# One direction per head group instead of two: regrouping the graph-attention heads of a fused fp32 kernel

## The chip, the core and the metric

The kernel runs on one core of a Trainium2 chip. The metric is device time in microseconds (us) of one launch. The engines are TensorE (PE, matrix products, with its weight loads listed apart as PEld), VectorE (DVE), ScalarE (ACT), GpSimd (POOL) and SyncE (SP), which here issues transfers.

## What is computed

Two layers are applied in a row to x of 2 x 2048 x 512 fp32. The first is a transformer block (adaptive layer norm, 16-head attention over 2048 rows, a feed-forward part). The second is a graph attention, and it is the one that the change touches. For each of two directions d, every row attends to the first 20 rows of its batch, with 16 heads of 32 features:

```python
kv = self_feat[:, :ng]                                   # ng = 20
qh = (self_feat @ Wq.T + bq).reshape(B, N, H, dh)
kh = (kv @ Wk.T + bk).reshape(B, ng, H, dh)
aff = jnp.einsum('bnhd,bmhd->bnhm', qh, kh) * (1.0 / np.sqrt(dh))
aff = jnp.where(mask, aff, NEG) + label_bias[:, :, None, :]
w = jax.nn.softmax(aff, axis=-1)
out_t = jnp.einsum('bnhm,bmf->bnhf', w, kv)
out = jnp.einsum('bnhf,hgf->bnhg', out_t, Wout) + bout.reshape(H, F // H)
...
for d in range(2):
    output = output + _gat_attention(...)                # W, mask and bias of direction d
return exp_v + jax.nn.relu(output)
```

## The kernel before

The program is one long list of instructions for each engine, written out by hand; semaphores order the engines against each other. Its stages are the projections, the attention, the output projection, the feed-forward part, a lead-in of the graph attention (`*_graph_shared`) and then the graph attention itself (`*_graph`) in 32 tiles of 128 rows. The first stages take the time up to about 2915 us and are the same in both kernels, apart from a few small POOL instructions behind the last of them.

The lead-in folds the weights. `out_t` is linear in kv, so for each head the 20 rows of kv times that head's block of Wout can be made once: a matrix `vw` of (head, direction, node) rows by 32 columns per head. A tile then needs only softmax weights times `vw`. Several heads are done in one matmul: `vw` is block-diagonal over the heads of a group, its off-diagonal part cleared by a mask `bm`. A group of `HG` before is 3 or 2 heads with both directions, 40 rows per head (120 or 80 rows, 96 or 64 columns); six groups make 16 heads.

To build `vw` (`VW` loop of `pe_graph_shared`, L1468), kv is laid out in `kvr` with zeros for the other direction, and each group is eight matmuls: four for the weights of direction 0 (`woT`) and four for those of direction 1 (`wcT`). Twelve groups (two batches of six) are made, three after each of the four blocks of `pe_gg`, which make the folded scores (L1427, L1436, L1439). DVE masks each group from a PSUM bank into `vw` (L1510); two banks take turns.

In a tile t the PE does, in this order: scores of tile t+1 (`pe_score`, L1598 and L1602), the transposes of tile t's softmax weights (`pe_turn_w`, L1623), the transposes of x of tile t+2 (L1581), the linear part of tile t+1 (`pe_self`, L1611 and L1613), a small transpose (L1588) and the heads of tile t (`pe_heads`, L1632): weights transposed in `wT` as the stationary operand, `vw` as the moving one. Between scores and transposes lies the softmax: DVE adds the edge term and takes the maximum (L1747, L1753), POOL subtracts (L1798), ACT takes exp (L1700), DVE sums and inverts (L1758, L1762), POOL scales (L1801). ACT copies the transposed weights to `wT` (`act_turn_w`, L1680), and DVE adds the tile's result to x (L1768).

The score tile is laid out as (head, direction, node) before. Scores and the linear part are in fp32r, a single pass; the heads, `vw` and the folding are in fp32. The trace records each fp32 matmul as two matmuls with a weight load each, so the six heads matmuls of a tile stand there as x12, and eight of a `VW` group as 16.

Of the kernel before, what the change touches and what calls it, by code (L numbers as in the profile page):

```python
# [17 lines left out]
NK = D // 128  # L18
# [13 lines left out]
TRI = ((0, 0), (0, 1), (1, 0))  # L32
HG = ((0, 3), (3, 3), (6, 3), (9, 3), (12, 2), (14, 2))
EARLY = 84
# [113 lines left out]
def program(nc, a):  # L148
# [16 lines left out]
    with ExitStack() as ctx:  # L165
# [865 lines left out]
        rows = early("rows", 4, B, D + 640, dt=F32R)  # L1031
        brow, bm = early("brow", 3, D), early("bm", 120, 96)
        wbB, m4, sel, onb = early("wbB", 128, 12), early("m4", 128, 4), early("sel", 4, 2), early("onb", 3, 4)
# [4 lines left out]
        khT = early("khT", 128, 2, NK, NB)  # L1038
        kvr = early("kvr", 128, 2, B, NK, 3, 2, NG)
        khb = early("khb", 128, 2, B, NK, 4 * NG)  # L1040
# [55 lines left out]
        def pe_graph_start(f):  # L1096
# [27 lines left out]
            elif f in (7, 8):  # L1124
                b = f - 7
                if b == 0:
                    pe.wait_ge(s_prep, 5)
                    pe.wait_ge(s_qtc, 1)
                else:
                    pe.wait_ge(s_kv, 3)  # L1130
                for k in range(NK):
                    pe.matmul(ps[0:4, 7 - b, :], lc[:, b, k, :], wcT[:, k, :], start=(k == 0), stop=False)
                pe.matmul(ps[0:4, 7 - b, :], onb, brow, start=False, stop=True).then_inc(s_rowm, 1)
            elif f == 9:
                pe.wait_ge(s_rlo, 1)
                pe_kh(0, 7)
            elif f in (10, 11):
                for kin in (2 * f - 20, 2 * f - 19):
                    if kin == 0:
                        pe.wait_ge(s_rlo, 4)  # L1140
                    elif kin == 1:
                        pe.wait_ge(s_kh, 2)
                    elif kin == 2:
                        pe.wait_ge(s_gmd, 1)
                    else:
                        pe.wait_ge(s_gma, 1)
                    pe_gm(0, 0, kin, 6 + kin % 2)
# [148 lines left out]
        def pool_graph_start(f):  # L1296

            if f == 1:
                pool.memset(lc[:, :, :, 2:4], 0.0).then_inc(s_prep, 1)
                pool.memset(lq, 0.0).then_inc(s_prep, 1)  # L1300
                pool.memset(lb[:, :, :, 0:2], 0.0).then_inc(s_prep, 1)
                pool.memset(kvr.rearrange("p d b k h e n -> p (d b k h e n)"), 0.0).then_inc(s_prep, 1)
            elif f == 2:
                pool.wait_ge(s_small, 16 * NSMALL)
                pool.tensor_copy(lc[:, :, :, 0:2], condT2.rearrange("p k b -> p b k").unsqueeze(3)
                                 .to_broadcast([128, B, NK, 2])).then_inc(s_prep, 1)
                pool.tensor_copy(lb[:, :, :, 2:4], colb[:, 1:3, :].unsqueeze(3)
                                 .to_broadcast([128, 2, NK, 2])).then_inc(s_prep, 1)
            elif f == 6:
                kvT4 = kvT.rearrange("p k (b n) -> p k b n", b=B)  # L1310
                pool.wait_ge(s_kv, 3)
                pool.wait_ge(s_prep, 4)
                for b in range(B):
                    for d in range(2):
                        pool.tensor_copy(kvr[:, d, b, :, :, d, :], kvT4[:, :, b, :].unsqueeze(2)
                                         .to_broadcast([128, NK, 3, NG])).then_inc(s_prep, 1)
                pool.tensor_copy(lq[:, :, :, 0:2], qtT.rearrange("p k b -> p b k").unsqueeze(3)
                                 .to_broadcast([128, B, NK, 2])).then_inc(s_prep, 1)
                pool.wait_ge(s_prep, 11)
                for b in range(B):  # L1320
                    pool.tensor_copy(lq[:, b, :, 2:4], colb[:, 0, :].unsqueeze(2)
                                     .to_broadcast([128, NK, 2])).then_inc(s_prep, 1)
# [83 lines left out]
        wvp = place("wvp", [128, 2, NK, D], held, F32R)  # L1406
        vw = place("vw", [120, B, 6, 96], held + 16384)
        after_vw = held + 16384 + 4 * B * 6 * 96
        gg = [place(f"gg{b}", [128, 2, NK, 640], at2 + 24576 + 20480 * b, F32R)[:, :, :, :] for b in range(B)]
        GM = [(0, 1, k, (5, 6, 7, 5)[k]) for k in range(NK)] + [(1, n // 4, n % 4, 4 + n % 3) for n in range(8)]  # L1410
        VW = [(b, q) for b in range(B) for q in range(6)]

        def pe_gg(d, b):
            n = 2 * d + b
            if n == 0:
                pe.wait_ge(s_gma, 2)
                pe.wait_ge(s_gmd, 2)
                pe.wait_ge(s_cw_nat, n_cw)
                pe.wait_ge(s_prep, 13)
            else:  # L1420
# [22 lines left out]
        def pe_graph_shared():  # L1443
            ff_over(pe)
            pe_kh(1, 4)
            for n, (d, b, kin, bank) in enumerate(GM):
# [4 lines left out]
                pe_gm(d, b, kin, bank)  # L1451
            for nv, (b, q) in enumerate(VW):
                if nv % 3 == 0:
                    pe_gg(nv // 6, nv // 3 % 2)
                h0, nh = HG[q]
                rr, cc, i = 40 * nh, 32 * nh, 4 + nv % 2
                if nv == 0:
                    pe.wait_ge(s_gmd, 8)
                    pe.wait_ge(s_prep, 10)
                    pe.wait_ge(s_cw_o0, n_cw)  # L1460
                    pe.wait_ge(s_cw_o1, 16)
                if nv == 1:
                    pe.wait_ge(s_gma, 8)
                if nv >= 2:
                    pe.wait_ge(s_vw, nv - 1)
                for d in range(2):
                    for k in range(NK):
                        m = pe.matmul(ps[0:rr, i, 0:cc], kvr[:, d, b, k, 0:nh, :, :], woT[d][:, k, 32 * h0:32 * h0 + cc],  # L1468
                                      start=(d == 0 and k == 0), stop=(d == 1 and k == 3))
                m.then_inc(s_vwm, 1)  # L1470
# [20 lines left out]
        def dve_graph_shared():  # L1491
# [6 lines left out]
            dve.tensor_tensor(wvp[:, 1, :, :], wvT, wvp[:, 0, :, :].bitcast(F32), ALU.subtract).then_inc(s_wvl, 1)  # L1498
            for nv, (of, q) in enumerate(VW):
                n = nv // 3  # L1500
                d, b = divmod(n, 2)
                if nv % 3 == 0:
                    for kv_ in range(NK):
# [3 lines left out]
                    dve_rows(2 + n, b, 6 + b, D + 320 * d, 320)  # L1507
                rr, cc = 40 * HG[q][1], 32 * HG[q][1]
                dve.wait_ge(s_vwm, nv + 1)
                dve.tensor_tensor(vw[0:rr, of, q, 0:cc], ps[0:rr, 4 + nv % 2, 0:cc], bm[0:rr, 0:cc],  # L1510
                                  ALU.mult).then_inc(s_vw, 1)
# [104 lines left out]
        def pe_turn_w(t):  # L1616
            pe.wait_ge(s_w, t + 1)
            for i in range(2):
                if t:
                    pe.wait_ge(s_wT, 3 * (t - 1) + 2 * i + 1)  # L1620
                for q in range(3):
                    h0, nh = HG[3 * i + q]
                    m = pe.transpose(ps[0:40 * nh, 5 + i, 128 * q:128 * q + 128],  # L1623
                                     ex[:, t % 2, 40 * h0:40 * (h0 + nh)], ident[:, :])
                m.then_inc(s_tw, 1)

        def pe_heads(t):
            b, j = t // (NT // B), t % 2
            for q, (h0, nh) in enumerate(HG):
                if q % 3 == 0:  # L1630
                    pe.wait_ge(s_wT, 3 * t + 2 * (q // 3) + 1)
                m = pe.matmul(ps[:, 3 + j, 32 * h0:32 * (h0 + nh)], wT[0:40 * nh, j, q, :],  # L1632
                              vw[0:40 * nh, b, q, 0:32 * nh], start=False, stop=(q == 5), skip_group_check=True)
            m.then_inc(s_hd, 1)
# [40 lines left out]
        def act_turn_w(t):  # L1675
            for r0, q0, q1 in ((120, 0, 3), (120, 3, 4), (80, 4, 6)):
                act.wait_ge(s_tw, 2 * t + q0 // 3 + 1)
                if t >= 2:
                    act.wait_ge(s_hd, t - 1)
                act.activation(wT[0:r0, t % 2, q0:q1, :],  # L1680
                               ps[0:r0, 5 + q0 // 3, 128 * (q0 % 3):128 * (q0 % 3 + q1 - q0)].rearrange(
                                   "p (q n) -> p q n", n=128), ACT.Copy).then_inc(s_wT, 1)

# [55 lines left out]
        def dve_soft1(t):  # L1739
            j = t % 2  # L1740
            a4 = af[:, j, :].rearrange("p (h d m) -> p h d m", d=2, m=NG)
            dve.wait_ge(s_score, 2 * t + 2)
# [3 lines left out]
            for d in range(2):  # L1746
                dve.tensor_tensor(a4[:, :, d, :], ps[:, 1 + d, 0:320].rearrange("p (h m) -> p h m", m=NG),  # L1747
                                  c2[:, j, 20 * d:20 * d + 20].unsqueeze(1).to_broadcast([128, H, NG]),
# [91 lines left out]
def lay_out(i):  # L1840
    g = {k: np.asarray(v) for k, v in i.items()}
    mask = g["mask_BxSxSx11_ik0"]
    adj = np.stack([mask[:, :, :NG, :], mask[:, :NG, :, :].transpose(0, 2, 1, 3)], axis=2)
    bm = np.zeros((120, 96), np.float32)
    for h in range(3):
        bm[40 * h:40 * h + 40, 32 * h:32 * h + 32] = 1.0
    m4 = np.zeros((128, 4), np.float32)
# [38 lines left out]
```

## Time and profile before

| what | value |
|---|---|
| median of 3 runs | 3323.95 us (3314.75 to 3324.57) |
| the profiled execution's own time | 3324.57 us |
| its span | 3323.3 us |
| PE busy over the span | 3203.7 us, 96% |
| DVE, ACT, POOL busy | 62%, 42%, 44% |
| mean granted clock of the PE | 0.98 of full speed |
| lead-in of the graph attention | 2929.4 to 2993.9 us |
| 29 of its 32 tiles | 3016.88 to 3306.5 us |

Busy shares are means over stages. Whether an engine sets the time of a stage is read from the chain of work that ended last, which is followed back from the last instruction: a piece of that chain is time that nothing else hid. The granted clock is the share of full speed that the PE was given; it has two levels, 2.4 GHz (1.00) and 1.2 GHz (0.50), and a value between them is a stretch with some of both.

### The profile page before, as it was taken

How to read it: one execution, taken by the hardware profiler on the slowest of the kernel's cores; microseconds unless marked ns; L12 is line 12 of the kernel's file. 1: busy time of each engine (PE TensorE's matmuls, PEld its weight loads, DVE VectorE, ACT ScalarE, POOL GpSimd, SP SyncE). 2: the span in 40 equal slices, each digit the busy share in tenths (PEclk: the TensorE clock that was granted, in tenths of full speed). 3: DMA queues.
4: the chain of work that ended last, by engine and by line, in shares of the span. 5: the costliest groups of instructions: out<-in, count | busy, mean ns of one | idle time of the engine just before them, and what ended most of it. 6: DMA issues, size and time to landing. Idle time of an engine off the chain costs nothing.

```text
span 3323.3 us, 44389 instructions
## 1 busy us (share of the span) xinstructions
PE 3203.7 (96%) x16890; PEld 2185.3 (66%) x16890; DVE 2072.6 (62%) x3524; ACT 1394.6 (42%) x2707; POOL 1471.1 (44%) x665
## 2 busy tenths in 40 slices
PE   8799999999999999999999996899999999999999
PEld 7677655555555555555555533678888888778888
DVE  4647778778788787887878753833333333226766
ACT  2121466666666666666666663311111111112322
POOL 0200478768777777787777865400000000002222
PEclk9899999999999999999999998999999999999999
DMA  5474588888979888798797857801111111311221
GB/s 196 147 220 138 146 202 186 190 193 187 210 175 204 194 179 203 180 203 194 175 197 186 180 135 205 288 19 39 38 39 39 38 38 40 102 34 64 73 77 58
DMA packets 186171, 466.22 MB, mean 140 GB/s; under 512 B 27196, under 2 KB 69308, under 8 KB 154215
## 3 DMA queue, kind: packets, MB, share of 16 engines
q0 software_dynamic: 32256, 234.90, 31.7%
q1 hardware_dynamic: 153703, 228.49, 23.2%
q8 instruction: 133, 2.18, 0.3%
q14 instruction: 79, 0.65, 0.1%
HBM read 151.90 MB, written 75.76 MB: 69 GB/s over the span
## 4 chain that ended last, share of the span: by engine, by line
PE 84%; DMA 8%; DVE 4%; issue 1%; ACT 1%; POOL 1%; SPq 0%; DVEq 0%; POOLq 0%; ACTq 0%
PE ps L359 13%; PE ps L621 13%; PE ps L633 12%; PE ps L1075 11%; PE ps L1064 11%; DMA accd<-pt 5%; PE ps L433 4%; PE ps L1598 3%; PE ps L639 3%; PE ps L1611 3%; PE ps L437 2%; PE ps L1632 1%; PE ps L937 1%; PE ps L1427 1%; ACT pt L689 1%
## 5 line engine op out<-in xcount | busy, mean ns | idle before, releaser
L372 DVE TENSOR_REDUCE nmp<-ps 128x1 f32<-128x512 f32 x1966 | 1202.2, 682 | 168.7 <-PE ps L359 167.2
L689 ACT ACTIVATE pt<-ps 128x512 f32<-128x512 f32 x2048 | 1034.5, 627 | 564.1 <-PE ps L621 563.6
L777 POOL TENSOR_TENSOR pacc<-pacc,pt 128x2048 f32<-128x2048 f32 x192 | 909.9, 4739 | 46.9 <-ACT pt L689 41.9
L621 PE MATMUL ps<-qs,ks 128*128 128x512 f32 x2048 | 824.6, 405 | 5.4 <-issue 3.2
L359 PE MATMUL ps<-ks,qs 96*128 96x512 f32 x1966 | 812.1, 413 | 8.7 <-DVE nmp L372 5.4
L359 PEld LDWEIGHTS ps<-ks,qs 96*128 96x128 f32 x1966 | 377.8, 192 | 277.3 <-DVE nmp L372 167.4
L633 PE MATMUL ps<-pt,vq 128*32 128x512 f32 x4096 | 495.6, 602 | 0.0
L621 PEld LDWEIGHTS ps<-qs,ks 128*128 128x128 f32 x2048 | 394.2, 193 | 106.2 <-ACT pt L689 25.0
L1064 PE MATMUL ps<-hpb,w 128*128 128x512 f32 x1536 | 380.3, 397 | 3.3 <-DMA x_d<-x 3.3
L1075 PE MATMUL ps<-w,gp 128*128 128x512 f32 x1536 | 380.5, 396 | 2.8 <-DVE gp L1208 2.8
L1075 PEld LDWEIGHTS ps<-w,gp 128*128 128x128 f32 x1536 | 289.4, 189 | 72.0 <-DVE gp L1208 3.2
L1064 PEld LDWEIGHTS ps<-hpb,w 128*128 128x128 f32 x1536 | 287.9, 189 | 69.3 <-issue 5.5
L1206 DVE CAST gp<-g 128x512 fp32r<-128x512 f32 x128 | 63.2, 494 | 406.7 <-ACT g L1198 406.7
L1198 ACT ACTIVATE g<-ps,b1c 128x512 f32<-128x512 f32 x128 | 88.1, 688 | 540.7 <-PE ps L1064 540.7
L633 PEld LDWEIGHTS ps<-pt,vq 128*32 128x32 f32 x4096 | 107.5, 109 | 248.3 <-ACT pt L689 166.2
L1330 POOL TENSOR_TENSOR res<-res,b2B 128x512 f32<-128x512 f32 x32 | 41.1, 1314 | 476.0 <-DMA res<-x_d 476.0
L108 POOL TENSOR_SCALAR ve<-mv 128x4 f32<-128x4 f32 x16 | 3.6, 228 | 411.1 <-DVE mv L103 411.1
L777 POOL TENSOR_TENSOR pacc<-pt 128x2048 f32<-128x2048 f32 x32 | 147.0, 4594 | 36.7 <-ACT pt L689 36.7
L763 POOL DMA_DIRECT2D accd<-pt x160 | 149.5, 935 | 9.2 <-ACT pt L689 8.9
L767 POOL DMA_DIRECT2D accd<-pt x64 | 37.3, 583 | 256.0 <-PE ps L639 189.4
L467 ACT ACTIVATE st<-ps,bqk 128x512 fp32r<-128x512 f32 x64 | 44.0, 688 | 236.3 <-PE ps L433 236.2
L714 DVE COPY accs<-ps 128x512 f32<-128x512 f32 x32 | 22.1, 692 | 191.8 <-PE ps L639 191.8
(169 smaller groups left out, 3166.3 us busy)
## 6 DMA issues: line engine op xcount, KB each, us to landing
accd<-pt POOLq DMA_DIRECT2D x224, 1024.0 KB, 8.8
qk_d<-st SPq DMA_DIRECT2D x128, 256.0 KB, 2.7
ks<-qk_d SPq DMA_DIRECT2D x24, 1024.0 KB, 17.2
qs<-qk_d SPq DMA_DIRECT2D x96, 256.0 KB, 6.7
xina<-in_x SPq DMA_DIRECT2D x8, 1024.0 KB, 6.3
v_d<-vst SPq DMA_DIRECT2D x32, 256.0 KB, 2.3
vq<-v_d SPq DMA_DIRECT2D x8, 1024.0 KB, 13.9
recb<-r_d SPq DMA_DIRECT2D x32, 256.0 KB
```

The lines of the kernel that those rows point to most:

```text
L359: pe.matmul(ps[:, ring.bank["max", u], :], qsb[0:96, v % 3, hq // 4, 128 * (hq % 4):128 * (hq % 4) + 128], ksb[w % 2][0:96, hq // 4, CH * ...
L372: dve.tensor_reduce(nmp[:, n // 4, n % 4:n % 4 + 1], ps[:, ring.bank["max", u], :], AX.X, ALU.max, negate=True).then_inc(s_mr, 1)
L433: m = pe.matmul(ps[:, bank, :], w[:, x, k, col:col + 128], hp[:, y, k, :], start=(i == 0 and k == 0), stop=(i == 2 and k == NK - 1))
L621: pe.matmul(ps[:, n % 3, :], ksb[w % 2][:, hh, 128 * kt:128 * kt + 128], qsb[:, v % 3, hh, :], start=True, stop=True).then_inc(s_sc, 1)
L633: m = pe.matmul(ps[32 * hh:32 * hh + 32, 7, :], vq[:, w % 2, kt, 32 * hh:32 * hh + 32], pt[:, g % 8, hh, :], start=(kt == 0), stop=(kt == 15))
L639: m = pe.matmul(ps[32 * hh:32 * hh + 32, bank, :], ones[:, :], src[:, hh, :], start=start, stop=stop)
L689: act.activation(pt[:, g % 8, hh, :], ps[:, n % 3, :], ACT.Exp, scale=SCALE).then_inc(s_exp, 1)
L763: pool.dma_start(accd[:, j % 2, :, :], pt[:, g % 8, :, :], accum_op=ALU.add).then_inc(s_dma[j % 2], 16)
L777: pool.tensor_tensor(pacc[:, :, :], first, pt[:, g % 8, :, :], ALU.add).then_inc(s_add, 1)
L1064: m = pe.matmul(ps[:, 4 + r, :], w1[:, f // 4, x, k, 128 * (f % 4):128 * (f % 4) + 128], hp[:, y, k, :], start=(i == 0 and k == 0), stop=( ...
L1075: m = pe.matmul(ps[:, t, :], gp[:, q % 2, x, 128 * t:128 * t + 128], w2[:, f // 4, y, f % 4, :], start=(i == 0 and f == 0), stop=(i == 2 a ...
L1598: pe.matmul(ps[:, 1 + d, 0:320], xp[:, j, x, 128 * k:128 * k + 128], gg[b][:, y, k, 320 * d:320 * d + 320], start=(i == 0 and k == 0), sto ...
```

## The change

Each group now holds one direction. `HG` becomes three groups of 6, 5 and 5 heads, 20 rows per head (120 or 100 rows, 192 or 160 columns), and each is done for both directions: six matmuls per tile as before. The score tile becomes (direction, head, node). `kvr` holds kv six times without zeros, so its memset goes and four copies become two. In the lead-in a group needs the weights of its own direction alone, four matmuls instead of eight. ACT copies `wT` in four pieces instead of three, since rows 120 and 100 alternate, and the waits count accordingly.

```diff
-HG = ((0, 3), (3, 3), (6, 3), (9, 3), (12, 2), (14, 2))
+HG = ((0, 6), (6, 5), (11, 5))
...
-        brow, bm = early("brow", 3, D), early("bm", 120, 96)
+        brow, bm = early("brow", 3, D), early("bm", 120, 192)
-        kvr = early("kvr", 128, 2, B, NK, 3, 2, NG)
+        kvr = early("kvr", 128, B, NK, 6, NG)
...
-                pool.memset(kvr.rearrange("p d b k h e n -> p (d b k h e n)"), 0.0).then_inc(s_prep, 1)
...
                 for b in range(B):
-                    for d in range(2):
-                        pool.tensor_copy(kvr[:, d, b, :, :, d, :], kvT4[:, :, b, :].unsqueeze(2)
-                                         .to_broadcast([128, NK, 3, NG])).then_inc(s_prep, 1)
+                    pool.tensor_copy(kvr[:, b, :, :, :], kvT4[:, :, b, :].unsqueeze(2)
+                                     .to_broadcast([128, NK, 6, NG])).then_inc(s_prep, 1)
...
-        vw = place("vw", [120, B, 6, 96], held + 16384)
+        vw = place("vw", [120, B, 2, 3, 192], held + 16384)
-        VW = [(b, q) for b in range(B) for q in range(6)]
+        VW = [(d, b, t) for d in range(2) for b in range(B) for t in range(3)]
...
-                rr, cc, i = 40 * nh, 32 * nh, 4 + nv % 2
+                rr, cc, i = 20 * nh, 32 * nh, 4 + nv % 2
                 if nv == 0:
...
-                    pe.wait_ge(s_cw_o1, 16)
+                if nv == 6:
+                    pe.wait_ge(s_cw_o1, 16)
...
-                for d in range(2):
-                    for k in range(NK):
-                        m = pe.matmul(ps[0:rr, i, 0:cc], kvr[:, d, b, k, 0:nh, :, :], woT[d][:, k, 32 * h0:32 * h0 + cc],
-                                      start=(d == 0 and k == 0), stop=(d == 1 and k == 3))
+                for k in range(NK):
+                    m = pe.matmul(ps[0:rr, i, 0:cc], kvr[:, b, k, 0:nh, :], woT[d][:, k, 32 * h0:32 * h0 + cc],
+                                  start=(k == 0), stop=(k == 3))
...
-            for i in range(2):
+            for d in range(2):
                 if t:
-                    pe.wait_ge(s_wT, 3 * (t - 1) + 2 * i + 1)
-                for q in range(3):
-                    h0, nh = HG[3 * i + q]
-                    m = pe.transpose(ps[0:40 * nh, 5 + i, 128 * q:128 * q + 128],
-                                     ex[:, t % 2, 40 * h0:40 * (h0 + nh)], ident[:, :])
+                    pe.wait_ge(s_wT, 4 * (t - 1) + 2 * d + 2)
+                for q, (h0, nh) in enumerate(HG):
+                    m = pe.transpose(ps[0:20 * nh, 5 + d, 128 * q:128 * q + 128],
+                                     ex[:, t % 2, 320 * d + 20 * h0:320 * d + 20 * (h0 + nh)], ident[:, :])
...
-            for q, (h0, nh) in enumerate(HG):
-                if q % 3 == 0:
-                    pe.wait_ge(s_wT, 3 * t + 2 * (q // 3) + 1)
-                m = pe.matmul(ps[:, 3 + j, 32 * h0:32 * (h0 + nh)], wT[0:40 * nh, j, q, :],
-                              vw[0:40 * nh, b, q, 0:32 * nh], start=False, stop=(q == 5), skip_group_check=True)
+            for d in range(2):
+                pe.wait_ge(s_wT, 4 * t + 2 * d + 2)
+                for q, (h0, nh) in enumerate(HG):
+                    m = pe.matmul(ps[:, 3 + j, 32 * h0:32 * (h0 + nh)], wT[0:20 * nh, j, 3 * d + q, :],
+                                  vw[0:20 * nh, b, d, q, 0:32 * nh], start=False, stop=(d == 1 and q == 2),
+                                  skip_group_check=True)
...
-            for r0, q0, q1 in ((120, 0, 3), (120, 3, 4), (80, 4, 6)):
-                act.wait_ge(s_tw, 2 * t + q0 // 3 + 1)
+            for d in range(2):
+                act.wait_ge(s_tw, 2 * t + d + 1)
...
+                for r0, q0, q1 in ((120, 0, 1), (100, 1, 3)):
+                    act.activation(wT[0:r0, t % 2, 3 * d + q0:3 * d + q1, :],
+                                   ps[0:r0, 5 + d, 128 * q0:128 * q1].rearrange("p (q n) -> p q n", n=128),
+                                   ACT.Copy).then_inc(s_wT, 1)
...
-            a4 = af[:, j, :].rearrange("p (h d m) -> p h d m", d=2, m=NG)
+            a4 = af[:, j, :].rearrange("p (d h m) -> p d h m", d=2, m=NG)
```

The PE's row of instructions in the lead-in, at the first three `VW` groups; sizes are rows by columns of the result. Before:

```order
L1439 MATMUL ps<-khb,lb 4x80 x4
L1468 MATMUL ps<-woT_113,kvr 120x96 [waits s_qst7,s_cw_o1,s_prep,s_gmd]
L1468 MATMUL ps<-woT_113,kvr 120x96 x3
L1468 MATMUL ps<-wcT,kvr 120x96 x4
L1468 MATMUL ps<-woT_113,kvr 120x96 [waits s_gma]
L1468 MATMUL ps<-woT_113,kvr 120x96 x3
L1468 MATMUL ps<-wcT,kvr 120x96 x4
L1468 MATMUL ps<-woT_113,kvr 120x96 [waits s_vw]
L1468 MATMUL ps<-woT_113,kvr 120x96 x3
L1468 MATMUL ps<-wcT,kvr 120x96 x4
L1427 MATMUL ps<-gm_139,wnat 128x320 [waits s_ggl,s_gmd,s_gma]
```

and now, at the same place:

```order
L1437 MATMUL ps<-khb,lb 4x80 x4
L1466 MATMUL ps<-woT_113,kvr 120x192 [waits s_qst7,s_prep,s_gmd]
L1466 MATMUL ps<-woT_113,kvr 120x192 x3
L1466 MATMUL ps<-woT_113,kvr 100x160 [waits s_gma]
L1466 MATMUL ps<-woT_113,kvr 100x160 x3
L1466 MATMUL ps<-woT_113,kvr 100x160 [waits s_vw]
L1466 MATMUL ps<-woT_113,kvr 100x160 x3
L1425 MATMUL ps<-gm_139,wnat 128x320 [waits s_ggl,s_gmd,s_gma]
```

Twenty-four matmuls became twelve, each about twice as wide, and the wait on `s_vw` (DVE's mask step of the first group) stands nearer to the start.

The PE's row in a tile, from the small transpose to the next scores. Before:

```order
L1588 MATMUL ps<-ident,nzt 4x128 [waits s_zT,s_nzv]
L1632 MATMUL ps<-vw,wT 128x96 [waits s_wT]
L1632 MATMUL ps<-vw,wT 128x96 x2
L1632 MATMUL ps<-vw,wT 128x96 [waits s_wT]
L1632 MATMUL ps<-vw,wT 128x64 x2
L1598 MATMUL ps<-gg_143,xp 128x320 [waits s_af,s_xl]
```

and now:

```order
L1585 MATMUL ps<-ident,nzt 4x128 [waits s_zT,s_nzv]
L1628 MATMUL ps<-vw,wT 128x192 [waits s_wT]
L1628 MATMUL ps<-vw,wT 128x160 x2
L1628 MATMUL ps<-vw,wT 128x192 [waits s_wT]
L1628 MATMUL ps<-vw,wT 128x160 x2
L1595 MATMUL ps<-gg_143,xp 128x320 [waits s_af,s_xl]
```

The count and the waits stay; the columns of the six together go from 512 to 1024.

## Rows read from the trace of the kernel before

**Rows 1.** The page: the chain that ended last, shares by line.
```profile
PE ps L359 13%; PE ps L621 13%; PE ps L633 12%; PE ps L1075 11%; PE ps L1064 11%; DMA accd<-pt 5%; PE ps L433 4%; PE ps L1598 3%; PE ps L639 3%; PE ps L1611 3%; PE ps L437 2%; PE ps L1632 1%; PE ps L937 1%; PE ps L1427 1%; ACT pt L689 1%
```

**Rows 2.** Stretches: length, busy us of each engine (instructions), granted clock, DMA share, GB/s.
```profile
2929.40:2993.90 64.50, 64.45 (x384) 46.67 (x383) 17.98 (x41) 11.51 (x24) 0.10 (x1) 1.00 0.08 27
3016.88:3306.50 289.62, 289.62 (x1799) 248.19 (x1799) 201.82 (x378) 87.67 (x232) 73.95 (x58) 1.00 0.22 73
```

**Rows 3.** Chain that ended last, one tile: start us, us, what.
```profile
3136.72 3.57 PE ps L1598 x24
...
3142.01 2.78 PE ps L1611 x12
...
3145.42 1.29 PE ps L1632 x12
```

**Rows 4.** Instructions in time order, weight loads around the heads: start us, us, what.
```profile
3145.15 1.42 PEld L1632 LDWEIGHTS ps<-vw,wT 120*128 120x128 f32 x12
...
3146.48 1.62 PEld L1598 LDWEIGHTS ps<-gg,xp 128*128 128x128 f32 x11
```

**Rows 5.** Chain that ended last, in the lead-in.
```profile
2940.83 5.21 PE ps L1468 x48
2946.04 8.64 PE ps L1427 x32
...
2956.93 0.55 PE ps L1439 x8
2957.48 4.13 PE ps L1468 x48
```

**Rows 6.** Instructions in time order, weight loads in the lead-in.
```profile
2940.76 0.92 PEld L1468 LDWEIGHTS ps<-woT,kvr 128*120 128x120 f32 x8
...
2945.80 8.38 PEld L1427 LDWEIGHTS ps<-gm,wnat 128*128 128x128 f32 x32
...
2957.41 0.91 PEld L1468 LDWEIGHTS ps<-woT,kvr 128*120 128x120 f32 x8
...
2961.39 0.57 PEld L1427 LDWEIGHTS ps<-gm,wnat 128*128 128x128 f32 x3
```

**Rows 7.** Groups by line and shape in the lead-in: busy us, mean ns, idle before.
```profile
L1506 DVE TENSOR_TENSOR gg<-ps,gg 128x320 fp32r<-128x320 f32 x16 | 7.8, 490 | 25.5 <-ACT gg L1487 25.5
L1510 DVE TENSOR_TENSOR vw<-ps,bm 120x96 f32<-120x96 f32 x8 | 2.1, 258 | 5.7 <-PE ps L1468 5.7
```

**Rows 8.** Instructions in time order: DVE's first mask step.
```profile
2942.72 0.26 DVE L1510 TENSOR_TENSOR vw<-ps,bm 120x96 f32<-120x96 f32 x1
```

**Rows 9.** Instructions in time order, one tile: ACT's copies and POOL's scaling.
```profile
3141.28 0.92 ACT L1680 ACTIVATE wT<-ps 120x384 f32<-120x384 f32 x3 [5.55 <-PE ps L1623]
...
3147.70 1.28 POOL L1801 TENSOR_TENSOR ex<-ex,rc 128x640 f32<-128x640 f32 x1 [3.80 <-DVE rc L1762]
```

**Rows 10.** Chain that ended last, the next transposes of softmax weights.
```profile
3150.76 0.80 PE ps L1623 x6
```

**Rows 11.** Groups by line and shape in the tiles: the narrowest of ACT's copies.
```profile
L1680 ACT ACTIVATE wT<-ps 120x128 f32<-120x128 f32 x29 | 7.9, 271 | 0.0
```

**Rows 12.** Instructions in time order, the last tile, PE.
```profile
3314.44 1.55 PE L1632 MATMUL ps<-vw,wT 120*128 120x96 f32 x12
...
3317.09 0.87 PE L1623 MATMUL ps<-ident,ex 128*120 128x128 f32 x6 [1.10 <-POOL ex L1801]
```

**Rows 13.** Chain that ended last: first scores, last heads.
```profile
2997.83 5.05 PE ps L1598 x24
...
3318.22 2.23 PE ps L1632 x12
```

**Rows 14.** Stretches at the first scores and the last heads; columns as in rows 2.
```profile
2998.00:3000.00 2.00, 2.00 (x10) 2.00 (x10) 1.56 (x5) 1.78 (x3) 0.00 (x0) 0.52 0.47 121
...
3318.90:3320.50 1.60, 1.53 (x8) 1.34 (x7) 0.03 (x1) 0.00 (x0) 0.00 (x0) 0.51 0.00 0
```

More of the change, by code:

```diff
@@ L1126, in pe_graph_start @@
                 if b == 0:
-                    pe.wait_ge(s_prep, 5)
+                    pe.wait_ge(s_prep, 4)
                     pe.wait_ge(s_qtc, 1)
@@ L1311, in pool_graph_start @@
                 pool.wait_ge(s_kv, 3)
-                pool.wait_ge(s_prep, 4)
                 for b in range(B):
-                    for d in range(2):
-                        pool.tensor_copy(kvr[:, d, b, :, :, d, :], kvT4[:, :, b, :].unsqueeze(2)
-                                         .to_broadcast([128, NK, 3, NG])).then_inc(s_prep, 1)
+                    pool.tensor_copy(kvr[:, b, :, :, :], kvT4[:, :, b, :].unsqueeze(2)
+                                     .to_broadcast([128, NK, 6, NG])).then_inc(s_prep, 1)
+                pool.wait_ge(s_prep, 2)
                 pool.tensor_copy(lq[:, :, :, 0:2], qtT.rearrange("p k b -> p b k").unsqueeze(3)
                                  .to_broadcast([128, B, NK, 2])).then_inc(s_prep, 1)
-                pool.wait_ge(s_prep, 11)
+                pool.wait_ge(s_prep, 8)
                 for b in range(B):
@@ L1406, in program @@
         wvp = place("wvp", [128, 2, NK, D], held, F32R)
-        vw = place("vw", [120, B, 6, 96], held + 16384)
-        after_vw = held + 16384 + 4 * B * 6 * 96
+        vw = place("vw", [120, B, 2, 3, 192], held + 16384)
+        after_vw = held + 16384 + 4 * B * 2 * 3 * 192
         gg = [place(f"gg{b}", [128, 2, NK, 640], at2 + 24576 + 20480 * b, F32R)[:, :, :, :] for b in range(B)]
         GM = [(0, 1, k, (5, 6, 7, 5)[k]) for k in range(NK)] + [(1, n // 4, n % 4, 4 + n % 3) for n in range(8)]
-        VW = [(b, q) for b in range(B) for q in range(6)]
+        VW = [(d, b, t) for d in range(2) for b in range(B) for t in range(3)]
         def pe_gg(d, b):
@@ L1418, in pe_gg @@
                 pe.wait_ge(s_cw_nat, n_cw)
-                pe.wait_ge(s_prep, 13)
+                pe.wait_ge(s_prep, 10)
             else:
@@ L1451, in pe_graph_shared @@
                 pe_gm(d, b, kin, bank)
[L1452 to L1455, printed above, removed]
-                rr, cc, i = 40 * nh, 32 * nh, 4 + nv % 2
+            for nv, (d, b, t) in enumerate(VW):
+                if t == 0:
+                    pe_gg(d, b)
+                h0, nh = HG[t]
+                rr, cc, i = 20 * nh, 32 * nh, 4 + nv % 2
                 if nv == 0:
                     pe.wait_ge(s_gmd, 8)
-                    pe.wait_ge(s_prep, 10)
+                    pe.wait_ge(s_prep, 7)
                     pe.wait_ge(s_cw_o0, n_cw)
-                    pe.wait_ge(s_cw_o1, 16)
                 if nv == 1:
                     pe.wait_ge(s_gma, 8)
+                if nv == 6:
+                    pe.wait_ge(s_cw_o1, 16)
                 if nv >= 2:
                     pe.wait_ge(s_vw, nv - 1)
-                for d in range(2):
-                    for k in range(NK):
-                        m = pe.matmul(ps[0:rr, i, 0:cc], kvr[:, d, b, k, 0:nh, :, :], woT[d][:, k, 32 * h0:32 * h0 + cc],
-                                      start=(d == 0 and k == 0), stop=(d == 1 and k == 3))
+                for k in range(NK):
+                    m = pe.matmul(ps[0:rr, i, 0:cc], kvr[:, b, k, 0:nh, :], woT[d][:, k, 32 * h0:32 * h0 + cc],
+                                  start=(k == 0), stop=(k == 3))
                 m.then_inc(s_vwm, 1)
@@ L1498, in dve_graph_shared @@
             dve.tensor_tensor(wvp[:, 1, :, :], wvT, wvp[:, 0, :, :].bitcast(F32), ALU.subtract).then_inc(s_wvl, 1)
[L1499 to L1502, printed above, removed]
+            for nv, (d, b, t) in enumerate(VW):
+                n = 2 * d + b
+                if t == 0:
                     for kv_ in range(NK):
@@ L1507, in dve_graph_shared @@
                     dve_rows(2 + n, b, 6 + b, D + 320 * d, 320)
-                rr, cc = 40 * HG[q][1], 32 * HG[q][1]
+                rr, cc = 20 * HG[t][1], 32 * HG[t][1]
                 dve.wait_ge(s_vwm, nv + 1)
-                dve.tensor_tensor(vw[0:rr, of, q, 0:cc], ps[0:rr, 4 + nv % 2, 0:cc], bm[0:rr, 0:cc],
+                dve.tensor_tensor(vw[0:rr, b, d, t, 0:cc], ps[0:rr, 4 + nv % 2, 0:cc], bm[0:rr, 0:cc],
                                   ALU.mult).then_inc(s_vw, 1)
@@ L1675, in act_turn_w @@
         def act_turn_w(t):
-            for r0, q0, q1 in ((120, 0, 3), (120, 3, 4), (80, 4, 6)):
-                act.wait_ge(s_tw, 2 * t + q0 // 3 + 1)
+            for d in range(2):
+                act.wait_ge(s_tw, 2 * t + d + 1)
                 if t >= 2:
                     act.wait_ge(s_hd, t - 1)
-                act.activation(wT[0:r0, t % 2, q0:q1, :],
-                               ps[0:r0, 5 + q0 // 3, 128 * (q0 % 3):128 * (q0 % 3 + q1 - q0)].rearrange(
-                                   "p (q n) -> p q n", n=128), ACT.Copy).then_inc(s_wT, 1)
+                for r0, q0, q1 in ((120, 0, 1), (100, 1, 3)):
+                    act.activation(wT[0:r0, t % 2, 3 * d + q0:3 * d + q1, :],
+                                   ps[0:r0, 5 + d, 128 * q0:128 * q1].rearrange("p (q n) -> p q n", n=128),
+                                   ACT.Copy).then_inc(s_wT, 1)
         def act_graph():
@@ L1746, in dve_soft1 @@
             for d in range(2):
-                dve.tensor_tensor(a4[:, :, d, :], ps[:, 1 + d, 0:320].rearrange("p (h m) -> p h m", m=NG),
+                dve.tensor_tensor(a4[:, d, :, :], ps[:, 1 + d, 0:320].rearrange("p (h m) -> p h m", m=NG),
                                   c2[:, j, 20 * d:20 * d + 20].unsqueeze(1).to_broadcast([128, H, NG]),
@@ L1843, in lay_out @@
     adj = np.stack([mask[:, :, :NG, :], mask[:, :NG, :, :].transpose(0, 2, 1, 3)], axis=2)
-    bm = np.zeros((120, 96), np.float32)
-    for h in range(3):
-        bm[40 * h:40 * h + 40, 32 * h:32 * h + 32] = 1.0
+    bm = np.zeros((120, 192), np.float32)
+    for h in range(6):
+        bm[20 * h:20 * h + 20, 32 * h:32 * h + 32] = 1.0
     m4 = np.zeros((128, 4), np.float32)
```

## The prediction, made before the changed kernel ran

> **What bounds the kernel now.** I read the chain that ended last first, by line [rows 1]. The lines that the change touches are small there: L1632 is 1% of the span, L1468 is below the list. Whatever happens to them is a matter of a few tenths of a per cent, so the signs have to be worked out in nanoseconds per matmul.
>
> Then I read the two stretches where these lines stand [rows 2]. In the lead-in the PE is busy 64.45 of 64.50 us, in 29 steady tiles 289.62 of 289.62 us, both at a granted clock of 1.00. A tile takes 289.62 / 29 = 9.99 us, and DVE, the next busiest, is busy 201.82 / 29 = 7.0 us of it. So the PE is the bound at both places, and a nanosecond on it is a nanosecond of the kernel. The chain in time order says the same: within a tile it never leaves the PE [rows 3].
>
> Last I read what paces the short fp32 matmuls. Weight loads and matmuls alternate, and each can hide the other. In the heads the loads start at 3145.15 and the next line's at 3146.48, 1.33 us for 12, 111 ns each [rows 4]. Eight of these matmuls have 96 columns and four have 64, yet the pace is one. That is the mark of the weight load (128 columns) setting it, the matmul being shorter. In the lead-in I have fp32 matmuls that are clearly paced by their own columns: 320 columns at 8.64 / 32 = 270 ns, and 80 columns, with a load of only four, at 0.55 / 8 = 69 ns [rows 5]. Between the two a column costs (270 - 69) / 240 = 0.84 ns. So 192 columns take 69 + 112 x 0.84 = 163 ns, and 160 take 136 ns. Both are over the 111 ns of the load. The width of the groups, free up to now, will begin to be paid.
>
> **The change part by part.**
>
> *Heads, each tile.* Six fp32 matmuls are twelve in the trace. Now 1.33 us. Then 4 x 163 + 8 x 136 = 1.74 us, the load of 111 ns hidden behind each. That is +0.41 us; the starts in between are modelled to some ten ns, and I take +0.40. By ends the chain gives 1.29 us for the old twelve [rows 3], so the upper value by the same pace is +0.45. The heads of the last tile but one are hidden: they end at 3315.99 and the PE then sits idle 1.10 us for POOL [rows 12]. The last tile is counted below. So 30 tiles pay: 30 x 0.40 = **+12.0 us**.
>
> *The lead-in.* Here the pair of zero-padded directions goes, half of the matmuls. A block with three groups of three heads now takes 2945.80 - 2940.76 = 5.04 us, one with a group of three and two of two 2961.39 - 2957.41 = 3.98 us, from first load to the load of the next line [rows 6]. Each stands twice, 18.04 us. Then each of four blocks has eight matmuls of 192 columns and sixteen of 160: 8 x 163 + 16 x 136 = 3.48 us, together 13.92. That is **-4.1 us**. By the chain's pieces, 5.21 and 4.13, it would be -4.8 [rows 5], but these hold 0.17 us at the start of each block that is no pace of columns and stays.
>
> *The wait that moves nearer.* The third group of a block reuses the bank of the first and waits for DVE's mask. DVE is in order and was still at its rows when group one was ready; its mask begins at 2942.72 [rows 8]. A mask of 192 columns takes, between 258 ns for 96 and 490 for 320 [rows 7], about 358 ns, so it ends at 2943.08. The PE wants the bank at 2940.83 + 1.30 + 1.09 = 2943.22. That holds by 0.14 us, less the passing of a semaphore. I put 0.05 us a block, **+0.2 us**, with 0 and 2.0 (0.5 each) as ends. The mask after the last group, with 160 columns, is about 0.1 us longer and lies on the path to the first transposes: **+0.1 us**.
>
> *ACT and DVE in a tile.* Four copies in place of three for the same columns in all. The one more costs at most what a copy of 128 columns takes, 0.27 us [rows 11]. The three end at 3142.2 and the heads start at 3145.4, so that hides [rows 3, 9]. What comes behind them on ACT, and so the softmax, shifts by as much at most. POOL's last step ends at 3148.98, its reader starts at 3150.76, 1.8 us of room [rows 9, 10], and the longer tile adds 0.40. **0.** The score layout leaves every operation its size: 0. The memset that goes and POOL's copies lie under the feed-forward part; POOL is busy 0.10 us in the whole lead-in, so nothing waits for it [rows 2]: 0.
>
> *The last tile.* Its heads are bare, and most of them ran at half clock: 2.23 us, and 0.51 was granted from 3318.9 on [rows 13, 14]. The first 0.7 us were at full clock. New work of 1.74 us, 0.7 at full speed and 1.04 at half, is 0.7 + 2.1 = 2.8, against 0.7 + 2 x 0.63 = 2.0 for the old, so +0.8; the copies before it add 0.1 by the part of the 0.27 that isn't overlapped. **+0.9 us**, with 0.5 if the clock holds.
>
> *The clock at the first scores.* After the lead-in the PE waits for DVE and then runs its first scores in 5.05 us in place of 3.57, at 0.52 [rows 3, 13, 14]. The changed kernel arrives there 4 us earlier with the same gap. It can escape the drop (-1.5) or meet it as now. I take 0 with -1.5 as an end.
>
> Sum: +12.0 - 4.1 + 0.2 + 0.1 + 0.9 = **+9.1 us** on the profiled execution's 3324.57 us: **3333.7 us**. Its span is 3323.3, the 1.3 around it do not change. The median shown is 3323.95, so this is +0.29%. About 0.3% either way, 10 us, is what a measurement of this kernel can tell from no change, and my sum lies just under it.
>
> **The rivals.**
>
> *A fixed cost on each matmul (slower).* The fp32r rows are not at their columns' price: 3.57 / 24 = 149 ns for 320 columns and 2.78 / 12 = 232 ns for 512 [rows 3], 192 columns apart at 0.43 ns each, which leaves some 15 ns a matmul (149 - 320 x 0.417). If fp32 matmuls close to their load's length pay that as well, the heads are 4 x 175 + 8 x 149 = 1.89 us, +0.56 a tile, +16.8; a lead-in block is 8 x 175 + 16 x 149 = 3.78, together -2.9; with the 1.2 of the rest +15.1, **3339.7 us**, slower by 0.47%. Against it: the fp32 row of 320 columns, with the same load of 128, pays only 270 - 267. It decides from +0.43 us a tile on, where the total passes 10 us.
>
> *The load keeps the pace (not slower).* If the wider matmuls still hid behind their loads, the heads would stay at 1.33 us, and a lead-in block would go by loads: 105 ns for 120 columns (5.04 / 48), about 88 for 100 (between this and 72 for 80, from 3.98 = 16 x 0.105 + 32 x 0.072), 8 x 105 + 16 x 88 = 2.25 us, together -9.0. With +0.2 for the rest: **3315.8 us**, -0.25%. Against it speaks the 270 ns of 320 columns, which is over twice the load.
> The Trainium skill has a rule that would give this case (TensorE: Matmul & The Clock Gate, Back-to-back issue gap): in a stream of load and matmul pairs a matmul of 128 columns sustains about 81 ns and one of 512 about 131. By that, 160 and 192 columns are estimated at 85 to 89 ns, below the load. The trace here does not agree for fp32: 270 ns at 320 columns.
>
> *Another engine becomes the bound (slower).* If DVE's mask step holds the PE in each block for 0.5 us, and ACT's and DVE's longer chain eats the room in a tile, +2 us and more come on top: **3336 us**. For it: the margin of 0.14 us. Against it in the tiles: 1.8 us of room, which grows.
>
> **How the numbers follow.** Forecast 0.76; fixed cost 0.10; load's pace 0.05; another bound 0.09. The forecast's own range is 3329 to 3337: heads between 0.38 and 0.45 a tile, the clock's -1.5, and the runs of before that differ by up to 10 us among themselves. The rivals on the slow side reach 3340, those on the fast side 3316; leaving out under 2 in 10, 3326 to 3340. The forecast sits on the bound of 0.3%, so I split it, 0.39 within and 0.35 slower, 0.02 faster by a lucky clock. The fixed cost and the other bound go to slower (0.10 and 0.06, with 0.03 within), the load's pace to within 0.03 and faster 0.02. Together: faster 0.04, within 0.45, slower 0.51.
>
> **What would show it.** The steady tile at 10.39 us in place of 9.99, the heads' piece of the chain at 1.7 us, matmuls 163 and 136 ns apart, and weight loads with idle time between them. The lead-in shorter by 4 us, with `VW` blocks near 3.5 to 3.7 us and no PE idle named after DVE's mask. PE busy for the whole of the steady stretch. I would be wrong if the heads' pace stays near 111 ns, if it is above 1.8 us, or if the PE waits in a tile.

## The result, and the profile after

| | kernel before | changed kernel |
|---|---|---|
| median, first comparison (6 runs each) | 3324.94 us (3314.75 to 3334.52) | 3343.39 us (3340.17 to 3361.20) |
| ratio, with its 95% interval | | 1.0055 [1.0034, 1.0078] |
| profiled execution: its time, its span | 3324.57, 3323.3 us | 3342.29, 3341.0 us |
| mean of all runs, all comparisons | 3336.7 us (114 runs, standard error 0.8) | 3345.1 us (56 runs, standard error 1.1) |

The forecast was 3333.7 us in a range of 3326 to 3340. The time came out above the range. The last line of the table takes in the later comparisons; it gives +8.4 us with a standard error of 1.3, where the forecast's sum was +9.1. How far that line can be trusted is said with the experiments.

I took the profile after in the order of the forecast's terms. First the chain that ended last for one steady tile: start us, us, what. It answers to rows 3 (L1598, L1611, L1632 are now L1595, L1608, L1628).

```profile
3137.31 3.52 PE ps L1595 x24
...
3147.70 3.52 PE ps L1595 x24
3151.22 0.48 PE ps L1599 x2
3151.70 0.80 PE ps L1619 x6
3152.51 0.44 PE ps L1578 x4
3152.94 2.78 PE ps L1608 x12
...
3156.35 1.74 PE ps L1628 x12
```

The scores of one tile start at 3137.31 and those of the next at 3147.70, so a tile takes 10.39 us. The twelve heads matmuls of that tile stand in the same chain, and their weight loads in the list in time order, which answers to rows 4:

```profile
3145.96 1.74 PE ps L1628 x12
```

```profile
3145.69 1.77 PEld L1628 LDWEIGHTS ps<-vw,wT 120*128 120x128 f32 x12
...
3147.41 3.55 PEld L1595 LDWEIGHTS ps<-gg,xp 128*128 128x128 f32 x24
```

From the first load to the load of the next line it is now 1.72 us, where it was 1.33. The stretches of the profile give the whole: columns as in rows 2, the first row is L1092 (untouched by the change), the second the 29 steady tiles.

```profile
2918.90:2939.50 20.60, 20.60 (x98) 20.60 (x98) 4.17 (x9) 2.19 (x5) 0.00 (x0) 0.50 0.01 2
3022.98:3324.39 301.41, 301.41 (x1801) 259.95 (x1800) 200.01 (x378) 89.75 (x261) 73.97 (x58) 1.00 0.21 70
```

The tiles went from 289.62 to 301.41 us, the PE busy without a gap. The lead-in shrank as computed; its blocks in the chain, answering to rows 5:

```profile
2952.14 3.66 PE ps L1466 x24
2955.80 8.61 PE ps L1425 x32
...
2967.21 3.66 PE ps L1466 x24
```

And there is what no term had: L1092, 96 narrow matmuls of the lead-in that both kernels issue alike, ran at a granted clock of 0.50. The chain of the changed kernel, and under it that of the kernel before:

```profile
2914.77 4.42 PE ps L1084 x32
2919.19 20.55 PE ps L1092 x96
```

```profile
2914.89 3.74 PE ps L1084 x32
2918.62 10.75 PE ps L1092 x96
```

The two kernels reach L1084 at 2914.77 and 2914.89, so up to there they differ by 0.12 us. Then the changed kernel loses 11.4 us at unchanged work: 0.7 in L1084, 9.8 in L1092 and 0.9 in the first block of L1425 behind it (9.60 us, where L1427 took 8.66 in the kernel before). That, with 8 from the changed parts less 1.5 that the first scores gain by a full clock, is the 17.7 us between the two spans.

### The profile page after: what moved, and what is told of

It is laid out like the page before. It is cut to its first block, busy times and chain, and to the rows that moved or that the text cites. A ratio compares the mean times of both kernels' runs of the same rounds, so it can differ in the third digit from the quotient of the medians.

```text
span 3341.0 us, 44195 instructions
## 1 busy us (share of the span) xinstructions
PE 3222.9 (96%) x16794; PEld 2203.2 (66%) x16794; DVE 2069.4 (62%) x3524; ACT 1395.4 (42%) x2739; POOL 1470.4 (44%) x662
## 4 chain that ended last, share of the span: by engine, by line
PE 84%; DMA 8%; DVE 4%; issue 2%; ACT 1%; POOL 1%; SPq 0%; DVEq 0%; POOLq 0%; ACTq 0%
PE ps L359 13%; PE ps L621 12%; PE ps L633 12%; PE ps L1075 11%; PE ps L1064 11%; DMA accd<-pt 6%; PE ps L433 4%; PE ps L1595 3%; PE ps L639 3%; PE ps L1608 3%; PE ps L437 2%; PE ps L1628 2%; PE ps L937 1%; PE ps L1425 1%; ACT pt L689 1%
## 5 line engine op out<-in xcount | busy, mean ns | idle before, releaser
L1064 PE MATMUL ps<-hpb,w 128*128 128x512 f32 x1536 | 381.9, 398 | 3.3 <-DMA x_d<-x 3.3
L1075 PE MATMUL ps<-w,gp 128*128 128x512 f32 x1536 | 380.5, 396 | 2.2 <-DVE gp L1208 2.2
L1075 PEld LDWEIGHTS ps<-w,gp 128*128 128x128 f32 x1536 | 289.4, 188 | 71.5 <-DVE gp L1208 2.7
L1064 PEld LDWEIGHTS ps<-hpb,w 128*128 128x128 f32 x1536 | 289.0, 190 | 69.8 <-issue 5.5
```

Of the source, the lines that this page charges most:

```text
L1064: m = pe.matmul(ps[:, 4 + r, :], w1[:, f // 4, x, k, 128 * (f % 4):128 * (f % 4) + 128], hp[:, y, k, :], start=(i == 0 and k == 0), stop=( ...
L1075: m = pe.matmul(ps[:, t, :], gp[:, q % 2, x, 128 * t:128 * t + 128], w2[:, f // 4, y, f % 4, :], start=(i == 0 and f == 0), stop=(i == 2 a ...
```

## The experiments

Two theories stood at the start. **A**: the sum over the changed parts holds (+8 to +9 us), and the rest is a drop of the PE's clock at L1092 that either kernel meets in part of its runs. **B**: the drop comes with the change. Times below are means with their standard errors, since single executions of one kernel lie up to 47 us apart. Each experiment was profiled once.

L1092 is only a part of that spread. In the nine profiles that leave the stages ahead of L1084 as they are, in either kernel, L1084 begins between 2914.4 and 2930.5 us, so 16 us come from the stages before. What makes them differ was not looked for. The profile from which the forecast was made was among the earliest there (2914.89) and was spared at L1092 too.

**The kernel before, unchanged (no edit).**

> The kernel before, run again unchanged, to see how its time spreads and at which clock its stretch of short matmuls at L1092 runs. Theory A (my sum holds, and the 10 us beyond it are a drop of the PE's clock at L1092 that either kernel meets by chance): ratio 1.000, and among the before runs some are 10 us longer, as 3334 against 3324. Theory B (the drop at L1092 comes with the changed code, regularly): the times of before stay near 3324, and L1092 takes 10.8 us at full clock here.

Measured: ratio 0.9993 [0.9974, 1.0012]; 12 runs, mean 3337.1 us (3327 to 3355), and the 35 runs of before beside them 3338.5 +- 1.3. So the time of before is not 3325 but about 3337. This execution took 21.2 us more than the one of the forecast: 10.1 were lost before L1084, the rest behind it. The chain of this execution, in the lead-in:

```profile
2924.09 0.93 issue
2925.02 4.50 PE ps L1084 x32
2929.52 20.55 PE ps L1092 x96
```

and the stretch of L1092:

```profile
2929.30:2949.80 20.50, 20.50 (x98) 20.50 (x98) 4.17 (x9) 2.19 (x5) 0.00 (x0) 0.50 0.01 2
```

The same row, 20.5 us at 0.50, in the kernel without the change. Theory B falls: the drop does not need the change. Whether the change makes it more frequent is not shown: of the unmodified kernels, before had it in one profile of two, the changed one in four of four.

**The changed kernel, three more groups of runs (no edit).**

> The changed kernel again. Theory A: ratio between 1.002 and 1.005; if the profile shows L1092 at full clock (10.8 us), the stretch from its start to the end of the program is about 8.5 us longer than before's, if at half clock (20.6 us) about 19 us longer. Theory B: ratio 1.0055 again and L1092 at half clock again, 20.6 us.

> The changed kernel once more, for the mean over many runs. Theory A: mean 8 us above the kernel before in the same session, within 3 us of uncertainty, ratio 1.0025. If the first comparison (1.0055) was right and my sum wrong: 18 us, 1.0055.

> The changed kernel, a fourth group of runs. Over all groups so far its mean is 8.1 us above the kernel before (44 runs against 85), while single groups gave 0 to 18. Theory A: this group lies between 3336 and 3353, and the mean over all stays at 7 to 10 us above. If a group had a level of its own (placement in memory, say), its spread would be small against its distance from the other groups.

Measured: 3340.3 +- 3.2 us (12 runs, ratio 0.9999 [0.9978, 1.0020]), 3349.8 +- 1.0 (9 runs, 1.0051 [1.0030, 1.0072]), 3347.3 +- 1.8 (12 runs, 1.0031 [1.0014, 1.0047]). L1092 took 19.9, 20.0 and 20.6 us in their profiles. The steady tiles took 10.39 us in each. From the start of L1092 to the end of the span the first of them took 420.8 us, 16.1 more than the kernel before at full clock (404.7). About 19 had been expected: this drop took 9.8 us in L1092 and its neighbours, not 11.4, and the first scores escaped theirs.

One comparison alone gave anything between nothing and half a per cent; over all of them the changed kernel is 8.4 +- 1.3 us slower, ratio 1.0025. But the four groups of the changed kernel lie 20, 2, 14 and 9 us above the runs of before beside them, further apart than single errors of 2 to 4 us let one expect. So a group seems to have a level of its own, the standard errors here are too small, and the four groups alone would give 11 +- 4. That 8.4 comes so near to the sum is partly luck. What tests the sum is the profiles, part by part.

**Nine wide matmuls ahead of L1092, in both kernels.**

```diff
             pe_kh(1, 4)
+            for _ in range(9):
+                pe.matmul(ps[:, 0, :], wkT[0][:, 0, 0:128], wkT[0][:, 1, :], start=True, stop=True)
```

> The kernel before with nine fp32 matmuls of 512 columns, whose result nobody reads, between L1084 and L1092. They are 18 passes of about 430 ns, 7.7 us, and wide enough that the clock should be at full when L1092 starts. Both theories: L1092 takes 10.8 us, total 7.7 us over before's runs without a drop, ratio 1.002. A third, C (the rest is no matter of the clock), says nothing else of it.

> The changed kernel with the same nine matmuls. L1092 at full clock in both. Theories A and B: 8.5 us longer than the kernel before with them (-4.1 lead-in, +12.2 tiles, rest 0.4), ratio to the kernel before 1.005. Theory C: 18 us longer, ratio 1.0078.

Measured: 3334.4 +- 1.5 us and 3344.8 +- 1.7 us, 10.4 us apart (ratios to the kernel before 0.9996 [0.9977, 1.0014] and 1.0013 [0.9995, 1.0030]). Of the kernel before with them, the chain:

```profile
2920.84 4.34 PE ps L1084 x32
2925.18 10.56 PE ps L1447 x18
2935.74 10.68 PE ps L1092 x96
```

The nine took 10.6 us, not 7.7, because the drop now falls on them (granted clock 0.50 from 2925.2 to 2930.0); behind them L1092 ran in 10.68 us, in the changed kernel too. The kernel before took 10 us of extra work and was not longer in the mean (3334.4 against 3338.5 +- 1.3). That speaks for a drop in most of its runs, which the extra work spares L1092. Between the two kernels the difference is that of the sum, within its error of 2.3, and far from theory C's 18.

The profiles of this pair give the changed parts cleanly, since L1092 and the lead-in behind it are at full clock in both. The first block and the last `VW` block before:

```profile
2946.42 8.66 PE ps L1427 x32
...
3006.78 4.14 PE ps L1470 x48
```

and in the changed kernel:

```profile
2939.95 8.66 PE ps L1425 x32
...
2951.41 3.66 PE ps L1468 x24
...
2996.64 3.68 PE ps L1468 x24
```

By ends that is 64.50 and 60.37 us, -4.13. From the start of L1092 to the end of the span the two take 402.4 and 412.5 us, 10.2 apart. Of that, 1.5 is the first scores, which met the drop in the changed kernel alone (5.06 us at 0.66, against 3.52 at 1.00). So 8.6 us are the price of the change at equal clock in this pair: 12.2 in the tiles, -4.1 in the lead-in and 0.45 in the last heads (2.02 and 1.57 us).

**Half the columns in the heads.**

```diff
-                    m = pe.matmul(ps[:, 3 + j, 32 * h0:32 * (h0 + nh)], ...
-                                  vw[0:20 * nh, b, d, q, 0:32 * nh], ...
+                    m = pe.matmul(ps[:, 3 + j, 32 * h0:32 * h0 + 16 * nh], ...
+                                  vw[0:20 * nh, b, d, q, 0:16 * nh], ...
```

> The changed kernel whose heads matmuls move half of their columns, 96 and 80 instead of 192 and 160; it leaves out the other half of each head group's output. Theory A (the price is 163 and 136 ns a matmul by its columns, and below 111 ns the weight load sets the pace): the heads of a tile take 1.33 us again, a tile 9.99 us in place of 10.39, the whole 12.2 us less than the changed kernel and 3.7 us less than the kernel before, all at equal clock. Rival E (a fixed cost on each of the matmuls): 0.1 to 0.2 us more than that a tile.

Measured: the chain of a tile,

```profile
3137.44 3.56 PE ps L1595 x24
...
3146.12 1.30 PE ps L1628 x12
3147.43 3.56 PE ps L1595 x24
```

9.99 us from scores to scores, 1.30 for the heads, as in the kernel before, with the same twelve matmuls and loads. So columns above what the load hides are the whole price, 0.41 us a tile, and rival E (a fixed cost on each matmul) falls. The time itself says less: 3334.0 +- 2.2 us, 1.4 under the 3335.5 +- 1.5 of before in its session, where 3.7 was expected; its L1092 ran at half clock (20.0 us).

**The narrow matmuls interleaved with wide ones, in both kernels.** L1084 of direction 1 moves up to the feed-forward part, and L1092 is mixed with the first block of L1427.

```diff
+            elif f == 14:
+                pe.wait_ge(s_gma, 2)
+                pe_kh(1, 7)
...
-            ff_over(pe)
-            pe_kh(1, 4)
             for n, (d, b, kin, bank) in enumerate(GM):
+                if n == 2:
+                    pe.wait_ge(s_kht, 2)
+                if n == 3:
+                    ff_over(pe)
+                if n in (3, 5, 8, 10):
+                    pe_gg(0, 0, (3, 5, 8, 10).index(n))
```

> The kernel before with L1084 for direction 1 moved up among the wide matmuls of the feed-forward part, the first groups of L1092 started without the wait for its last results, and the rest of L1092 interleaved with the first block of L1427 (320 columns). Same work. Theory A (a chance drop of the PE's clock at a long row of narrow matmuls costs either kernel 10 us in a part of its runs): the row is broken up, half clock there is rare, the mean of the runs goes down by 4 to 8 us and the slowest runs vanish. Rival D (the spread comes from the stages before 2880 us alone): the mean goes down by at most the 1 us gap that is filled, the spread stays.

> The changed kernel with the same moves. Theory A: 8.5 us longer than the kernel before with them, as the sum over its parts says (-4.1 lead-in, +12.2 tiles, +0.4), ratio between the two 1.0025. If a cost beyond this sum came with the change, the difference would be 12 us or more.

> The kernel before with the narrow matmuls interleaved, once more, since its first comparison (3330.1 mean against 3335.5) was not clear of the spread. Theory A: mean 4 to 8 us below the kernel before again, and below the changed kernel by 12 or more. Rival D (no gain but the filled gap): within 2 us of the kernel before.

Measured: before with them 3330.1 +- 1.8 and again 3332.0 +- 1.9 us, against 3335.5 +- 1.5 and 3338.0 +- 1.4 for the kernel before beside them (0.9987 [0.9966, 1.0007] and 0.9981 [0.9963, 0.9998]). The second group lies 15 us under the changed kernel of its session, where 12 or more were expected. The changed kernel with them 3335.2 +- 2.4, so 5 +- 3 us above its pair, which fits 8.5 and doesn't test it. One of the five mixed pieces of L1092 in the chain of the first:

```profile
2932.61 2.64 PE ps L1092 x24
```

110 ns a matmul, full clock, and so for all of them in the three profiles. The gain is 5.7 us in the mean, and rival D, which allowed 1 us, is unlikely. The slowest runs fell from 3352 and 3350 to 3341 and 3339, but a spread of 22 us remained, which the stages ahead can give.

The gain is the clock alone. From the start of the last 24 matmuls of L1075 to the end of the last `VW` block, the stretch that the moves rearrange takes 85.5 us in the kernel before at full clock, 96.9 at half clock, and 86.0 in the second profile of the mix, where the PE filled the gap but then waited 1.5 us for DVE's first mask:

```profile
2908.34 5.61 PE ps L1075 x24
2913.96 0.93 issue
...
2989.73 4.14 PE ps L1468 x48
```

```profile
2922.53 2.80 PE ps L1075 x12
...
3004.39 4.14 PE ps L1488 x48
```

**Only L1084 moved, L1092 left as it was, in the kernel before.**

```diff
+            elif f == 14:
+                pe.wait_ge(s_gma, 2)
+                pe_kh(1, 7)
...
-            pe_kh(1, 4)
```

> The kernel before with only L1084 for direction 1 moved up; L1092 stays one row of 96 narrow matmuls behind the 1 us gap. Theory F (the gap and the 40-column row of L1084 make the clock drop; L1092, once begun at full clock, keeps it, as in the first profile and behind the nine wide matmuls): L1092 runs in 10.8 us. Theory G (L1092's own narrow matmuls behind a gap do): 19.8 us or more in part of it.

Measured: 3330.9 +- 2.0 us against 3338.0 +- 1.4, ratio 0.9978 [0.9962, 0.9993]. The chain and the stretch:

```profile
2919.87 3.50 PE ps L1084 x32
2923.37 2.89 PE ps L1075 x12
2926.26 1.01 issue
2927.27 10.91 PE ps L1092 x96
```

```profile
2927.30:2938.10 10.80, 10.80 (x97) 10.80 (x98) 2.95 (x6) 2.19 (x5) 0.00 (x0) 1.00 0.16 60
```

Behind the gap alone, and with the 40-column row of L1084 moved away, L1092 kept the full clock. That speaks for theory F, that the gap with L1084 behind it makes the drop. It is one profile; the mean of twelve runs, 7 us lower, suggests that most runs do so. The move is faster in the mean than both kernels, and the mix does no more. A changed kernel with it wasn't run.

The gap is not needed for a drop. An earlier L1084, of direction 0, stands in all thirteen profiles between wide matmuls, with no gap ahead. In four of them the clock fell right behind it. The two cases:

```profile
2877.89 3.50 PE ps L1084 x32
2881.39 4.41 PE ps L1064 x12
```

```profile
2876.14 3.50 PE ps L1084 x32
2879.64 2.84 PE ps L1064 x12
```

The first (half the columns in the heads) had a clock of 0.61 over L1064, the second is the kernel before. The same happened once behind the moved L1084, in the first profile of the mix (L1075 4.24 us in place of 2.88). Followed by wide matmuls such a drop cost 1.4 to 1.6 us, followed by L1092 9.8 to 11.5.

Over all profiles: with L1084 and L1092 in their places and nothing between them, L1092 ran at full clock in one of seven, the very one that the forecast was made from. With the wide matmuls, the mix or the move it did so in all six.

## Why the prediction was wrong

*The base.* The forecast was 3324.57 us plus the sum. This step failed. The profiled execution, and the six of the first comparison, lay low in a spread that later runs put at 3310 to 3357 with a mean of 3336.7. I took the profiled time because the median of three runs agreed with it; that these three lay 10 us apart should have told me that neither stood for the kernel. With 3336.7 for the base the same sum gives 3345.8, and the changed kernel's mean is 3345.1, though the groups scatter too much for this to be a test. The 12 us by which the base was low are not the drop at L1092 alone: that profile was also early at L1084.

*The clock.* I looked for a clock drop only where the profile showed one, at the first scores, and gave it -1.5. The rows at full clock (2929.4 to 2993.9, 1.00) I took as given. L1092, just ahead of them, is where the clock fell in six profiles of seven. A drop there costs 9.1 to 9.8 us in L1092 (20.55 less 10.75) and with its neighbours up to 11.5, more than the whole sum. The forecast had no term for it; its place is in the range, on the upper side, since the base had been spared.

*The heads, +12.0.* Right. 301.41 - 289.62 = 11.79 for 29 tiles and 0.4 for the one outside that stretch, 12.2. 163 and 136 ns by interpolation gave 1.74 us, and 1.74 stands in the chain.

*The lead-in, -4.1.* Right, -4.13. The chain's own pieces (5.21 and 4.13 to 3.66, each twice: -4.0) would have given it too: they hold a start-up part on both sides.

*The wait that moves nearer, +0.2, and the last mask, +0.1.* Not there. In time order, DVE's masks and the PE's loads around them:

```profile
2952.06 3.47 PEld L1466 LDWEIGHTS ps<-woT,kvr 128*120 128x120 f32 x24
...
2954.03 0.34 DVE L1507 TENSOR_TENSOR vw<-ps,bm 120x192 f32<-120x192 f32 x1
2954.75 0.32 DVE L1507 TENSOR_TENSOR vw<-ps,bm 100x160 f32<-100x160 f32 x1 [0.39 <-PE ps L1466]
...
2955.50 1.67 PEld L1425 LDWEIGHTS ps<-gm,wnat 128*128 128x128 f32 x7
```

24 loads in 3.44 us with no idle time named, against 3.48 computed; the mask took 0.34 us, not 0.36, and the 0.14 us of room was enough. From the last `VW` matmul to the first transposes the chain takes 3.23 us, where it took 3.22, so the wider last mask cost 0.01.

*ACT and DVE in a tile, 0.* Right:

```profile
3141.82 0.99 ACT L1678 ACTIVATE wT<-ps 120x128 f32<-120x128 f32 x4 [5.95 <-PE ps L1619]
...
3148.25 1.27 POOL L1799 TENSOR_TENSOR ex<-ex,rc 128x640 f32<-128x640 f32 x1 [3.80 <-DVE rc L1760]
```

The copies take 0.99 us in place of 0.92 [rows 9]. POOL ends at 3149.52 and its reader starts at 3151.70, 2.2 us of room where there were 1.8.

*The last tile, +0.9, and the first scores.* Both went by the clock of that execution:

```profile
3005.01 3.52 PE ps L1595 x24
...
3336.12 2.02 PE ps L1628 x12
```

The last heads took 2.02 us, start included, at full clock [rows 13: 2.23], so this term was -0.2 in place of +0.9. At full clock in both kernels it is +0.45, near the 0.5 that the forecast gave for that case. The first scores escaped the drop, 3.52 for 5.05 us, as in the lower end of that term.

*The parts together.* 12.2 - 4.1 - 0.2 - 1.5 = +6.4 us in place of +9.1. Taken alone, these terms would have put the changed kernel lower than forecast. The 11.4 us around L1092, in no term, put it above the range.

*The rivals.* A fixed cost on each matmul: refuted, the heads stand at 1.74 and not 1.89 us. The load keeps the pace: refuted. The heads take 1.74 / 12 = 145 ns a matmul in the mean. That refutes, for fp32, the estimate of 85 to 89 ns from the Trainium skill (TensorE: Matmul & The Clock Gate, Back-to-back issue gap). Another engine as the bound: refuted, no gap on the PE.

*The first ratio, 1.0055.* It put 18 us on the change where 8 to 9 are its own by the profiles. 11 of the 18 in the two profiles are the drop at L1092. That the other runs of the first comparison divide in the same way is argued from their times, not shown; they were not profiled one by one.

## What to carry to other kernels

In this kernel the columns of a matmul are free while it is shorter than its weight load (111 ns for 128 columns). So wider groups gained where they make fewer matmuls (the lead-in, -4.1 us) and lost where the count stays (the tiles, +12.2 us). Before a change worth tenths of a per cent is priced, look at the spread of the runs and at the clock of the one execution: a row of narrow matmuls can run at either clock, and both prices belong in the range. Moving such rows in among wide matmuls was worth 6 to 7 us, nearly what this change cost.

## What the runs showed of the hardware

Of the seven profiles with the rows in their places, the clock dropped during L1084 (0.80 and 0.81 over it in two of them) or in the first microsecond of L1092 in six, and not at all in one. Once it had dropped, it stayed at 0.50 for the rest of the row, 20 us with the PE busy without a gap, and rose only under the 320-column matmuls behind it (0.91 over the first block in the changed kernel). So one row of 96 matmuls (80 columns, loads of 128) ran at either of two paces, 112 or 214 ns a matmul. The experiments point to what stands ahead of it as what decides: behind wide matmuls it kept the full clock in six profiles of six. A row of 32 matmuls of 40 columns was followed by a drop with a gap ahead of it and without one. Why it drops in one execution and not in another stays open.
